# Reordering VectorE and the SyncE queue, and both normalisations on ScalarE

## The reference

```python
q = exp(heads(x @ Wq.T + bq)); k = exp(heads(x @ Wk.T + bk)); v = heads(x @ Wv.T + bv)   # 16 heads of 32
kv = cumsum(k[..., None] * v[..., None, :], over tokens); k1 = cumsum(k, over tokens)
out = einsum('zsD,zsDd->zsd', q, kv) / sum(q * k1)
x = layernorm(x + out @ Wo.T + bo)                    # first normalisation, gives x1
x = layernorm(x + tanh(x @ weight @ aux_weight1 @ aux_weight2 + bias))   # second, gives the output
```

## Time and profile before

| | |
|---|---|
| runs | 2467.8 us median of 3 (2459.77 to 2468.61) |
| the profiled execution | 2467.03 us, of which the span of instructions is 2465.3 us |
| TensorE matmul busy | 94% |
| VectorE, GpSimd, ScalarE busy | 73%, 53%, 43% |
| mean granted TensorE clock | 0.992 of full |

### The profile page before, as it was taken

The page is one execution under the profiler, slowest core; times in us unless marked ns, Lnnn a source line. Parts: engine busy times, 40 slices in busy tenths (PEclk is TensorE's granted clock), DMA queues, the critical chain, the costliest instruction groups (busy, mean ns, idle before and its releaser), DMA issues.

```text
span 2465.3 us, 58596 instructions
## 1 busy us (share of the span) xinstructions
PE 2321.6 (94%) x21040; PEld 1907.9 (77%) x21040; DVE 1797.8 (73%) x2710; ACT 1052.8 (43%) x2039; POOL 1314.3 (53%) x1669
## 2 busy tenths in 40 slices
PE   6999999999999999999999999999999999999985
PEld 5778878877877887777777877777777877777764
DVE  4677777777777777777777777777777777777664
ACT  3434444444444444444444444444444444444431
POOL 1455555555655555555555555554555555555553
PEclk9999999999999999999999999999999999999998
DMA  6233333333333333333333333333333333333211
GB/s 162 71 98 103 106 99 102 103 98 96 105 100 100 103 100 97 104 98 99 102 97 100 102 99 100 102 99 99 99 101 100 100 102 99 98 103 96 64 65 52
DMA packets 293918, 241.90 MB, mean 98 GB/s; under 512 B 32848, under 2 KB 225360, under 8 KB 293712
## 3 DMA queue, kind: packets, MB, share of 16 engines
q1 hardware_dynamic: 293712, 238.69, 30.9%
HBM read 139.99 MB, written 98.57 MB: 97 GB/s over the span
## 4 chain that ended last, share of the span: by engine, by line
PE 93%; issue 4%; DVE 1%; ACT 1%; DMA 0%; SPq 0%; POOL 0%; POOLq 0%; ACTq 0%; DVEq 0%
PE G L310 25%; PE G L312 24%; PE G L311 24%; PE SC L377 6%; PE G L389 5%; PE G L364 4%; PE G L410 2%; PE G L401 1%; PE G L411 1%; PE SC L310 0%; PE SC L312 0%; PE SC L311 0%; DMA QT<-wqT 0%; DVE o L656 0%; SPq L272 0%
## 5 line engine op out<-in xcount | busy, mean ns | idle before, releaser
L775 POOL TENSOR_TENSOR qk1L<-WK,qk1H 128x512 fp32r<-128x512 f32 x128 | 165.4, 1292 | 814.7 <-ACT qk1H L555 814.7
L679 DVE RECIPROCAL o<-G 128x512 f32<-128x512 f32 x128 | 424.9, 3320 | 2.8 <-PE G L411 1.4
L673 DVE STREAM_TRANSPOSE SC<-WK 128x512 f32<-128x512 f32 x128 | 93.0, 727 | 448.5 <-DMA WK<-x_rows 448.5
L753 POOL TENSOR_SCALAR_AFFINE_SELECT A<-A 128x512 f32<-128x512 f32 x512 | 314.4, 639 | 10.7 <-issue 6.6
L517 ACT ACTIVATE A<-SC 128x512 f32<-128x512 f32 x512 | 275.3, 591 | 61.1 <-PE G L389 59.7
L792 POOL TENSOR_TENSOR xTL<-xin,xTH 128x512 fp32r<-128x512 f32 x128 | 164.8, 1288 | 245.6 <-ACT xTH L568 245.5
L310 PE MATMUL G<-WfH,x1H 128*128 128x512 f32 x512 | 211.1, 412 | 83.4 <-issue 71.7
L555 ACT ACTIVATE qk1H<-WK 128x512 fp32r<-128x512 f32 x128 | 81.0, 633 | 469.6 <-DVE WK L707 469.6
L724 DVE TENSOR_SCALAR WK<-xres,mv,rstd 128x512 f32<-128x512 f32 x128 | 200.5, 1566 | 86.4 <-POOL rstd L782 86.4
L533 ACT ACTIVATE x1H<-SC 128x512 fp32r<-128x512 f32 x128 | 76.6, 599 | 374.0 <-DVE SC L673 374.0
L310 PE MATMUL G<-xTH,WqH 128*128 128x512 f32 x512 | 203.0, 396 | 28.7 <-POOL xTL L792 21.1
(11 more groups left out here) (107 smaller groups left out, 5597.2 us busy)
## 6 DMA issues: line engine op xcount, KB each, us to landing
xin<-x SPq DMA_DIRECT2D x512, 64.0 KB, 1.9
xres<-x SPq DMA_DIRECT2D x128, 256.0 KB, 3.3
x_rows<-WK SPq DMA_DIRECT2D x128, 256.0 KB, 2.1
WK<-x_rows SPq DMA_DIRECT2D x512, 64.0 KB, 2.0
out<-WK SPq DMA_DIRECT2D x128, 256.0 KB, 2.1
k_rows<-WK SPq DMA_DIRECT2D x120, 256.0 KB, 2.3
WK<-k_rows SPq DMA_DIRECT2D x480, 64.0 KB, 2.0
QT<-wqT SPq DMA_DIRECT2D x4, 256.0 KB, 4.2
```

Source lines behind the costliest of these rows:

```text
L679: nc.vector.reciprocal(oflat, den_ps[:, :]).then_inc(recip_ready, 1)
L753: last = nc.gpsimd.affine_select(out=A[:, j, :, :], in_=A[:, j, :, :], compare_op=ALU.is_ge, fill=0.0, base=0, pattern=[[0, NK], [1, P]], ...
L775: nc.gpsimd.tensor_tensor(qk1L[:, :], WK[:, 7, :], qk1H[:, :].bitcast(F32), ALU.subtract).then_inc(qk1l_ready, 1)
```

## The change

It has three parts.

1. VectorE: the turn of tile k+8 (`x_turned`) moves from near the end of the slot to right behind the turn of the keys (`k_turned`), ahead of the reciprocal. The reciprocal moves ahead of the turn of `x1s`. Both normalisations leave VectorE.
2. SyncE: the store of the output moves behind the key transfers, and the load of `xres` moves behind the reload of `x1s`, with a wait for `x1_ready`.
3. ScalarE and GpSimd: GpSimd writes one more 128x1 value, `shift = -mean * rstd`, for each normalisation, and ScalarE computes `rstd * r + shift`. The second normalisation (tile k-3) stands on ScalarE between the state copies and the exponential of the keys; the first (tile k-1) stands behind Tanh.

```diff
@@ sync, slot @@
-                if c.exists(k - 3):
-                    n = k - 3
-                    wait_before(sp, (out_ready, c.count(n + 1)))
-                    sp.dma_start(out_t[n % B, c.it + n // B], y[:, n % 2, :]).then_inc(out_stored[n % B], 16)
                 if c.updates_state(k):
                     wait_before(sp, (k_turned, c.count(k + 1)))
...
+                if c.exists(k - 3):
+                    n = k - 3
+                    wait_before(sp, (out_ready, c.count(n + 1)))
+                    sp.dma_start(out_t[n % B, c.it + n // B], y[:, n % 2, :]).then_inc(out_stored[n % B], 16)
...
-                if c.exists(k + 1):
...
                 if c.exists(n):
                     wait_before(sp, (x1_stored[n % B], c.dma_count(n)), (x1_turned, c.count(n)))
...
+                if c.exists(k + 1):
...
+                    wait_before(sp, (x1_ready, c.count(k)))
+                    m = k + 1
+                    sp.dma_start(xres[:, m % 2, :], x_t[m % B, c.it + m // B]).then_inc(xres_loaded[m % B], 16)
@@ scalar, slot @@
+                if c.exists(k - 3):
+                    n = k - 3
+                    wait(act, shift2_ready, c.count(n + 1))
+                    nc.scalar.activation(y[:, n % 2, :], y[:, n % 2, :], ACT.Identity, bias=shift[:, 1:2],
+                                         scale=rstd[:, 1:2]).then_inc(out_ready, 1)
                 if proj:
                     wait(act, kproj_done, c.count(k + 5))
...
+                if prev:
+                    n = k - 1
+                    wait(act, shift1_ready, c.count(n + 1))
+                    wait(act, y_ready, c.count(n - 1))
+                    nc.scalar.activation(x1[:, n % 2, :], xres[:, n % 2, :], ACT.Identity, bias=shift[:, 0:1],
+                                         scale=rstd[:, 0:1]).then_inc(x1_ready, 1)
@@ vector, slot @@
+                if c.exists(k + 8):
+                    m = k + 8
+                    wait(dve, xin_loaded[m % B], c.part_count(m))
+                    xblocks = xin[:, m % XIN, :]
+                    nc.vector.transpose(xblocks, xblocks).then_inc(x_turned, 1)
...
-                if fin:
-                    wait(dve, rstd2_ready, c.count(k - 2))
-                    nc.vector.tensor_scalar(yf, yf, mv2[:, 0:1], rstd[:, 1:2],
-                                            ALU.subtract, ALU.mult).then_inc(out_ready, 1)
...
-                if prev:
-                    wait(dve, rstd1_ready, c.count(k))
-                    wait(dve, y_ready, c.count(k - 2))
-                    nc.vector.tensor_scalar(x1[:, (k - 1) % 2, :], r, mv1[:, 0:1], rstd[:, 0:1],
-                                            ALU.subtract, ALU.mult).then_inc(x1_ready, 1)
@@ gpsimd, slot @@
+                    wait_before(pool, (rstd1_ready, c.count(k)))
+                    nc.gpsimd.tensor_scalar(shift[:, 0:1], mv1[:, 0:1], rstd[:, 0:1], -1.0, ALU.mult,
+                                            ALU.mult).then_inc(shift1_ready, 1)
...
+                    wait_before(pool, (rstd2_ready, c.count(k - 1)))
+                    nc.gpsimd.tensor_scalar(shift[:, 1:2], mv2[:, 0:1], rstd[:, 1:2], -1.0, ALU.mult,
+                                            ALU.mult).then_inc(shift2_ready, 1)
```

More of the change, by code:

```diff
@@ L103, in linear_attention_ffn_kernel @@
         rstd = sb("rstd", [P, 2])
+        shift = sb("shift", [P, 2])
         mhalf = sb("mhalf", [P, 1])
@@ L128, in linear_attention_ffn_kernel @@
         scan_ready = sem("scan_ready")
+        shift1_ready, shift2_ready = sem("shift1_ready"), sem("shift2_ready")
         k1_ready = sem("k1_ready")
@@ L298, in slot @@
                                      x1_blocks[j]).then_inc(x1s_loaded[n % B], 16)
+                if c.exists(k + 1):
+                    if c.static() and c.it * B + k == -1:
+                        sp.wait_ge(c_done, 1)
+                    wait_before(sp, (x1_ready, c.count(k)))
+                    m = k + 1
+                    sp.dma_start(xres[:, m % 2, :], x_t[m % B, c.it + m // B]).then_inc(xres_loaded[m % B], 16)
             run_slots(sp, slot, 8, 3, {-7: load_wq_and_biases, -5: load_wk, -4: load_ffn_weights_and_wv,
@@ L571, in slot @@
                         ACT.Copy).then_inc(xh_ready, 1)
-            run_slots(act, slot, 8, 2, {-7: split_wq, -5: split_wk, -4: split_aux, -3: split_a12,
+            run_slots(act, slot, 8, 3, {-7: split_wq, -5: split_wk, -4: split_aux, -3: split_a12,
                                         -2: split_wv_wf_wo, -1: free_staging})
@@ L648, in slot @@
                 ffn = c.exists(k - 2)
-                fin = c.exists(k - 3)
                 oflat = o[:, :, :].rearrange("p g q -> p (g q)")
                 r = xres[:, (k - 1) % 2, :]
-                yf = y[:, (k - 3) % 2, :]
                 if prev:
@@ L667, in slot @@
                                         ).then_inc(k_turned, 1)
+                if c.exists(k + 8):
[3 more added lines that the diff above has]
+                    nc.vector.transpose(xblocks, xblocks).then_inc(x_turned, 1)
+                if att:
+                    wait(dve, den_done, c.count(k + 1))
+                    wait(dve, oh_ready, c.count(k))
+                    wait(dve, ol_ready, c.count(k))
+                    nc.vector.reciprocal(oflat, den_ps[:, :]).then_inc(recip_ready, 1)
                 if ffn:
@@ L674, in slot @@
                                         x1s[:, :].rearrange("p (t g f) -> p g t f", t=HG, f=HD)).then_inc(x1_turned, 1)
[L675 to L679, removed]
                 if ffn:
@@ L736, in slot @@
                     nc.vector.bn_aggr(mv2[:, :], bnst[:, 1, :]).then_inc(stats2_ready, 1)
-            run_slots(dve, slot, 8, 3, {-7: split_wq, -5: split_wk, -4: split_aux,
+            run_slots(dve, slot, 8, 2, {-7: split_wq, -5: split_wk, -4: split_aux,
                                        -3: split_a12, -2: split_wv_wf_wo, -1: add_bo})
```

## The result

The changed kernel takes 2953.2 us (median of 4 runs, 2949.5 to 2955.9); the kernel before takes 2464.6 us beside it. The ratio is 1.198, 95% interval 1.195 to 1.201. The forecast was 2846 us, in a range of 2690 to 2970.

A forecast was written before the change was run, and what follows sets the result against it. An 18.51 us ring through the store and reload of `x1` bounds, not TensorE (17.9). New ring 21.06 us over 118 slots: +301, keys +75, clock +18, last slots -15, together +379 us: forecast 2846 us, range 2690 to 2970.

The forecast's parts named there:

- The bound before: Steady slots: a ring from `x1` through its store and reload back to `x1`, 18.51 us; TensorE alone needs 17.9.
- What is removed: VectorE loses `x1` (1.61 us) and the second normalisation (0.5); reciprocal hidden, `xres` off the reload's path (1.2); ring 13.6 us.
- the load is there in time: Rival: `xin` lands before about 5 us, ring 13.6 us, TensorE's 17.9 bounds, 2380 us; chance 0.05.
- the keys' wait: VectorE's scan waits for ScalarE's exponential of the keys in every fourth slot: 2.5 us, some 30 slots, +75 us.
- The wait for `xin`: VectorE's turn of tile k+8 waits some 5 us in each of about 118 slots, 500 to 650 us in all.
- The transfer term: Ring part from the end of `x1` through SyncE's transfers to `xin` landed: 8.8 us, bounds 8.0 and 9.6.
- `shift`: New small GpSimd instruction in the ring: 0.30 us, plus 0.04 to cross to ScalarE; bounds 0.25 and 0.6.
- `x1` on ScalarE: First normalisation on ScalarE: 0.69 us against 1.61 on VectorE; bounds 0.60 and 0.85.
- The clock: Gaps lower TensorE's clock, slowing the feed-forward product: 0.15 us a slot, +18 us, bounds 0 and 41.
- The last slots: Last eight slots load no `xin`, so the change works as meant, with a 13.8 us ring in three: -15 us.
- The own case: The prediction's main case: ring of 20.1 to 22.3 us a slot, 2695 to 3020 us; chance 0.75.

The follow-up runs named there:

- the turn put back: Changed kernel with only the turn of tile k+8 back at its old place behind `z` on VectorE: 2465.5 us, ratio 0.999.
- the queue alone: Kernel before with only SyncE's new order, VectorE's and ScalarE's orders old and both normalisations on VectorE: 2447.3 us, ratio 0.991.
- the orders alone: Changed kernel with VectorE's and SyncE's new orders kept, both normalisations back on VectorE and `shift` dropped: 2931.5 us, ratio 1.186.
- the load put early: Changed kernel with SyncE loading tile k+9 in slot k behind the key transfers, except where that tile opens a chunk: 2552.7 us, ratio 1.034.
- GpSimd's small ones late: Changed kernel, turn of k+8 back, keys' exponential before second normalisation, GpSimd's second `ve`, `rstd`, `shift` behind next slot's masks: 2379.7 us, ratio 0.964.

## Why the prediction was right, and where it was short

- *The bound before.* Right: a ring of 18.5 us, with TensorE just below. With the normalisations moved and TensorE's work unchanged the slot fell to 17.67 us; with the queue's order alone the ring fell by 0.17 us and the slot by 0.16. TensorE's slot was read at least 0.2 us too long.
- *What is removed.* The sum for the ring if nothing else changed, 5.4 + 11.9 - 3.2 - 0.5 - 0.6, gives 13.0 us and not 13.6. The forecast does not hang on it, but the rival "the load is there in time" does: it had TensorE bound and the wait for the keys fit below it, for 2380 us. With the turn put back the load is in time, and the kernel takes 2465.5 us: the keys' wait adds its whole 2.5 us, and the third ring holds the other slots at 17.8 to 18.1. The 1.2 us for taking `xres` out of the reload's way have no run behind them either: the queue alone gave 0.17.
- *The wait for `xin`.* Right in place and nearly in size: "500 to 650 us", measured 577.7, with 569.7 from the orders alone. The turn put back takes all of the loss away, and the load put early takes the wait away in all slots but those where the load stays late.
- *The transfer term*, 8.8 us, measured 9.25: 0.45 us a slot or 53 of the missing 107 us. The four issues of a batch were taken at 1.84 us from one row; over all slots the reload took 2.25 (1.74 to 3.37) and `xin` 2.03, and the landing 1.70 instead of 1.52. With 0.24 for issues and gaps around `xres` that makes 1.02, of which I had covered 0.56 as a cost of `xres`. That the sum came so near is in part luck: the 0.56 stood for a cause that the runs do not bear out.
- *`shift`*: 0.30 forecast. It takes 0.27 and stands behind a gap of 0.17, and the statistics ahead of it start 0.12 us later than before: 0.56, or 31 us.
- *`x1` on ScalarE*: 0.69 from the nearest row, measured 0.81: 14 us. The Trainium skill (ScalarE: Activation LUTs, What ACT_TABLE_LOAD costs) charges each operand per partition, which had given an estimate of 0.80, the better one; the second normalisation shows the same 0.81.
- *The keys' wait*: 2.5 us forecast, 2.4 measured, in 31 slots. The price was right, the emphasis not: 1.85 of it come from the reciprocal's move and 0.6 from the normalisation.
- *The clock*: 0.15 us a slot forecast, 0.14 measured. Behind a gap of 4.79 us the feed-forward product ran at the lower level, 1.2 GHz: the window 1024 to 1026 us has this row, whose third number from the end is the granted clock.

```profile
1024.00:1026.00 2.00, 2.00 (x6) 1.52 (x6) 1.90 (x5) 1.88 (x3) 0.00 (x0) 0.50 0.06 24
```

  The sum `z` came late for it (the 0.64 us at 1027.57 above), and most of that was hidden behind `shift`. The Trainium skill (TensorE: Matmul & The Clock Gate, What's actually happening) has the clock fall when the engine idles. The trace agrees: the mean granted clock between 100 and 2700 us is 0.94, where it had been 1.00. The lower clock follows from the gaps, and costs 0.14 x 118 = 17 us.
- *The last slots*: -15 forecast, -0.7 measured. This is the step that failed in kind. "The change works as meant" there, I wrote, with a ring of 13.8 us. But the reciprocal waits for `oL` there, which the prediction did not see; after a first of 18.8 us the slots took 16.9 to 17.0 us, 19.4 to 19.5 with the wait for the keys, and 15.5 to 15.9 at the very end. The row that shows it, from the timeline of the changed kernel's VectorE at 2799 us:

```profile
2799.26 3.36 DVE L689 RECIPROCAL o<-G 128x512 f32<-128x512 f32 x1 [2.48 <-POOL oL L766]
```

With GpSimd's small ones late, slots of 17.03 and 17.04 us still stand there. In them `oL` follows `oH`, which follows `o`, and `o` waits for TensorE:

```profile
2294.80 0.69 DVE L668 TENSOR_TENSOR o<-G,o 128x512 f32<-128x512 f32 x1 [0.76 <-PE G L392]
2295.53 0.63 ACT L530 ACTIVATE oH<-o 128x512 fp32r<-128x512 f32 x1
2296.24 1.26 POOL L766 TENSOR_TENSOR oL<-o,oH 128x512 fp32r<-128x512 f32 x1
2297.63 3.36 DVE L684 RECIPROCAL o<-G 128x512 f32<-128x512 f32 x1 [2.14 <-POOL oL L766]
```

So in these slots the way to `oL` leads through TensorE's product for `o`, and not through GpSimd's list.

So 0.79 x 118 = 93 us of mis-sized terms and 14 in the last slots make up the 107 us between forecast and result. The own case had a ring of up to 22.3 us, to which the keys and the clock came on top, and the range held. Its top of 2970 us is only 17 us above the result.

## What to carry to other kernels

In a software pipeline, look for the chain that leaves a slot and comes back in the next, and sum it; a busy share of 94% does not say that the engine bounds. When an instruction is moved forward past a slow one, ask for each of its waits where the releaser stands in its own queue, not only how long the wait was in the old place: a wait of 5 us in all became 578 us because the place had hidden it. And an instruction that is taken from between two others was also a cover: the reciprocal had covered ScalarE's exponential and GpSimd's `oL`, and both came into the open.

## What the runs showed of the hardware

- An ACTIVATE of 128x512 with bias and scale per partition takes 0.81 us and one with a bias alone 0.67 to 0.69. With neither it takes 0.62 to 0.63 from SBUF and 0.59 to 0.60 from PSUM (`A`, `V`, `x1H`, whose source is `SC` or `G`); the two with a bias alone read PSUM too.
- The first normalisation on VectorE takes 1.61 us in nearly every slot beside GpSimd's sum of the same tile size, and 0.54 us where GpSimd does nothing. The rows of GpSimd for these two places:

```profile
1002.41 1.26 POOL L786 TENSOR_TENSOR WK<-WK 128x512 f32<-128x512 f32 x1
...
2428.93 1.29 POOL L786 TENSOR_TENSOR WK<-WK 128x512 f32<-128x512 f32 x1 [1.45 <-ACT WK L558]
```

  With the orders alone it took 1.05 us on average: 1.6 us in 60 tiles, all beside that sum, and 0.5 or 0.6 in the other 68, in 50 of which the sum did not run at all.
- Four DMAs of 64 KB issue in 1.74 us at best, and the reload of `x1` in up to 3.4. The long ones come also when nothing but a finished store is ahead of them, as the 3.37 us at 1009.09. What sets this is left open.
